# Row numbers by slot in a mixture-of-experts kernel: the tile index moved outside the slot column, 78 columns per product

## Chip, cores and metric

One Trainium2 chip, one core. The time is that of one execution on the device, in microseconds (us), from the median of several executions. Lower is better.

## What is computed

A conditioned layer in front of a mixture of experts, and then a stencil on its result. 2048 tokens of 256 features are normalised twice, scaled and shifted by a style, and routed: each token goes to the two best of eight experts. The part around the change works out only *which token goes where*. Cut to what matters:

```python
h_flat = h.reshape(-1, D)                          # 2048 tokens x 256
probs = softmax(h_flat @ router_w)                 # 8 experts
gates, idx = top_k(probs, 2)
gates = gates / gates.sum(-1, keepdims=True)
combine = zeros((N, E)).at[arange(N)[:, None], idx].add(gates)
hid = relu(einsum('nd,edf->nef', h_flat, exp_w1) + exp_b1)
eout = einsum('nef,efd->ned', hid, exp_w2) + exp_b2
x = x + einsum('ned,ne->nd', eout, combine)
# second layer: a stencil over the 256 x 256 field of each of 8 batches
df = -gradv_Af + gradvv_Bf * 0.5
out = maximum(x + df * dt, 0)
```

## The kernel before

**Stages.** (1) A front part of some 39 us normalises the tokens, turns them, applies the style and writes the result as rows to memory (`h_rows`); the router's logits fall out of the same products. (2) Routing, some 39 to 60 us: the two best experts of each token, its rank within its expert, the expert of each slot, and the row numbers that belong in each slot. (3) The experts: 23 slots, each one expert with up to two tiles of 128 rows. For each slot GpSimd gathers the rows (L731), TensorE turns them (L867) and runs two layers (L891/L893/L898 and L920), and GpSimd scatters the result (L744). The weights are split in a high and a low part by ScalarE and VectorE. (4) The stencil over four pairs of batches.

Each engine has its program written out by hand, with semaphores between them; nothing is reordered by a scheduler.

**The place of the change.** There are 32 tiles of routed tokens (`TOPK * NJ`, two choices times 16 tiles of 128 tokens) and 4992 slot places, 39 columns (`NC`) of 128 rows. At L1142 to L1146 VectorE has the place of each token as a column `col_f` and a row `low_f`. To turn *token to place* round into *place to token*, TensorE multiplies one-hot matrices:

- `oh_col` (L1155): is the column of the token this one? 39 x 32 numbers in each partition, compared with a table `col_of` that GpSimd's iota made (L721).
- `tok` has two halves: `tok[:, 0]` is `oh_col` times the token's number in its tile (ScalarE, L547), `tok[:, 1]` is `oh_col` times 128 times the tile's number (VectorE, L1158).
- `oh_row` (L1162): is the row this one? 128 x 32 numbers, in 4 chunks of 8 tiles.
- L854: for each tile `t` two products, `oh_row[:, :, t]` as weights and the two halves of `tok` at `t` as the 39 moving columns, all 64 added up in one place of PSUM. In all three arrays the tile is the *innermost* index, so that both operands of a product are read with a step of 32 numbers (64 bytes).

TensorE waits for `tok0_ok` (ScalarE), `tok_ok` (VectorE) and, once per 8 tiles, `ohrow_ok`. When all products are done (`perm_mm`), VectorE makes `num_i` and from it `src_cur`, the row numbers of the first two slots (L1169, L1170), on which GpSimd's first gather (L731) waits. `src_i` and `dst_i`, for the later slots, follow. `link` makes an instruction add to a semaphore and lets VectorE wait for it before its next one; `chained` only adds.

```python
dve.tensor_tensor(oh_col[:, :, :], by_tile(col_f[:, :], NC), col_of[:, :, :],
                  ALU.is_equal).then_inc(ohcol_ok, 1)
```

Of the kernel before, what the change touches and what calls it, by code (L numbers as in the profile page):

```python
# [7 lines left out]
ALU = mybir.AluOpType  # L8
# [112 lines left out]
def moe_then_stencil(nc, x, ids, dt, exp_w1, exp_b1, exp_w2, exp_b2, a_grid, b_grid, small, consts, out):  # L121
# [4 lines left out]
    with ctx:  # L126
# [29 lines left out]
        with ExitStack() as phase:  # L156
            def own(name, shape, dt_=F32):
                return phase.enter_context(nc.sbuf_tensor(name, shape, dt_))
# [15 lines left out]
        with ExitStack() as phase:  # L174
            def own(name, shape, dt_=F32):
                return phase.enter_context(nc.sbuf_tensor(name, shape, dt_))

            h_pre = own("h_pre", [P, KD, N])
            hT = own("hT", [P, KD, N])
            own("w_split_first", [P, 10240])  # L180

            z = own("z", [P, 4, D])
            tok = own("tok", [P, 2, NC, TOPK * NJ], BF16)
            own("w_split_last", [P, 6144 - 1024 - TOPK * NJ * NC])
            h_tok = own("h_tok", [P, NJ, KD, P + E])
            oh_row = own("oh_row", [P, P, TOPK * NJ], BF16)
            oh_col = own("oh_col", [P, NC, TOPK * NJ], BF16)
            eye_rw = own("eye_rw", [P, KD, P + E])
            before_bf = own("before_bf", [P, P], BF16)
            ones_bf = own("ones_bf", [P, P], BF16)  # L190
            st1 = own("st1", [P, NJ, 6])
            mv1 = own("mv1", [P, NJ, 2])
            var1 = own("var1", [P, NJ])
            rs1 = own("rs1", [P, NJ])
            st2 = own("st2", [P, NB, KD, 6])
            mv2 = own("mv2", [P, NB, KD, 2])
            var2 = own("var2", [P, NB, KD])
            rs2 = own("rs2", [P, NB, KD])
            half = own("half", [P, 8])
            warm = own("warm", [P, 8])  # L200
            aff_a = own("aff_a", [P, NB, KD])
            aff_m = own("aff_m", [P, NB, KD])
            aff_b = own("aff_b", [P, NB, KD])

            id_i = own("id_i", [S_SUB, NB], I32)
            id_f = own("id_f", [S_SUB, NB])
            oh_s = own("oh_s", [S_SUB, NB])
            small_sb = own("small_sb", [P, SMALL_ALL])
            se_t = own("se_t", [SE, NB])
            hy1 = own("hy1", [SH, NB])  # L210
            hy2 = own("hy2", [SH, NB])
            sy1 = own("sy1", [SH // 2, NB])
            sty = own("sty", [P, 4, NB])
            gabs = own("gabs", [P, KD, NB])
            grelu = own("grelu", [P, KD, NB])
            gexp = own("gexp", [P, KD, NB])
            gln = own("gln", [P, KD, NB])
            gsum = own("gsum", [P, KD, NB])
            gam = own("gam", [P, KD, NB])

            lg = own("lg", [P, NJ, E])
            eq = own("eq", [P, NJ, E])
            cand = own("cand", [P, NJ, E])
            least = own("least", [P, NJ])
            oh = own("oh", [P, TOPK, NJ, E])
            lg2 = own("lg2", [P, NJ, E])
            gap = own("gap", [P, NJ])
            e2 = own("e2", [P, NJ])
            den = own("den", [P, NJ])
            m_bf = own("m_bf", [P, NJ, E], BF16)  # L230
            cnt_i = own("cnt_i", [P, E], I32)
            tl_i = own("tl_i", [P, 2, E], I32)
            tl_f = own("tl_f", [P, 2, E])
            t_end = own("t_end", [P, 2, E])
            t_off = own("t_off", [P, 2, E])
            base = own("base", [P, E])
            room = own("room", [P, E])
            jump = own("jump", [P, E])
            late = own("late", [P, NJ, E])
            pos = own("pos", [P, NJ, E])  # L240
            pick = own("pick", [P, TOPK, NJ, E])
            slot_f = own("slot_f", [P, TOPK * NJ])
            slot_i = own("slot_i", [P, TOPK * NJ], I32)
            low_i = own("low_i", [P, TOPK * NJ], I32)
            col_i = own("col_i", [P, TOPK * NJ], I32)
            low_f = own("low_f", [P, TOPK * NJ], BF16)
            col_f = own("col_f", [P, TOPK * NJ], BF16)
            row_of = own("row_of", [P, P, TOPK * NJ], BF16)
            col_of = own("col_of", [P, NC, TOPK * NJ], BF16)
            tile_of = own("tile_of", [P, TOPK * NJ], BF16)  # L250
            e_cmp = own("e_cmp", [1, 2, NS, E])
            e_sum = own("e_sum", [1, NS])
            num_i = own("num_i", [P, NC], I32)
            num_f = own("num_f", [P, NC])

        def part(name):
            rows, cols, at = SMALL[name]
# [215 lines left out]
        def _(act):  # L473
# [66 lines left out]
            for b in range(3, NB):  # L540
# [3 lines left out]
            act.activation(e2[:, :], gap[:, :], ACT.Exp).then_inc(e2_ok, 1)  # L544

            act.wait_ge(ohcol_ok, 1)
            act.activation(tok[:, 0, :, :], oh_col[:, :, :], ACT.Copy,  # L547
                           scale=cst[:, C_PART + 1:C_PART + 2]).then_inc(tok0_ok, 1)

            def split_w1(k, m, first=False):  # L550
# [150 lines left out]
        def _(pool):  # L701
# [16 lines left out]
                    pool.tensor_tensor(rs2[:, i - 3, :], var2[:, i - 3, :], half[:, 0:KD],  # L718
                                       ALU.pow).then_inc(rs2_ok, 1)
            number(tile_of[:, :], [[P, TOPK * NJ]])  # L720
            number(col_of[:, :, :], [[1, NC], [0, TOPK * NJ]])  # L721
            number(row_of[:, :, :], [[1, P], [0, TOPK * NJ]])

            def gather(k, m):
# [48 lines left out]
        def _(pe):  # L773
# [76 lines left out]
            for t in range(TOPK * NJ):  # L850
                if t % CHUNK == 0:
                    pe.wait_ge(ohrow_ok, t // CHUNK + 1)
                for part in range(2):
                    last = pe.matmul(banks[1][:, 128:128 + NC], oh_row[:, :, t], tok[:, part, :, t],  # L854
                                     start=(t == 0 and part == 0), stop=(t == TOPK * NJ - 1 and part == 1))
            last.then_inc(perm_mm, 1)

            def turn(k, m):
# [114 lines left out]
        def _(dve):  # L973
            steps = [0]

            def link(ins):

                steps[0] += 1
                ins.then_inc(chain, 1)
                dve.wait_ge(chain, steps[0])  # L980
# [168 lines left out]
            TC = TOPK * NJ  # L1149

            def by_tile(v, n):
                return v.rearrange("p (a t) -> p a t", a=1).broadcast_to([P, n, TC])

            dve.wait_ge(iota_ok, 3)
            dve.tensor_tensor(oh_col[:, :, :], by_tile(col_f[:, :], NC), col_of[:, :, :],  # L1155
                              ALU.is_equal).then_inc(ohcol_ok, 1)
            dve.wait_ge(ohcol_ok, 1)
            dve.tensor_tensor(tok[:, 1, :, :], oh_col[:, :, :], by_tile(tile_of[:, :], NC),  # L1158
                              ALU.mult).then_inc(tok_ok, 1)
            for n in range(TC // CHUNK):  # L1160
                at = slice(CHUNK * n, CHUNK * n + CHUNK)
# [2 lines left out]
                    low_f[:, at].rearrange("p (a t) -> p a t", a=1).broadcast_to([P, P, CHUNK]), row_of[:, :, at],  # L1164
                    ALU.is_equal).then_inc(ohrow_ok, 1)
            dve.wait_ge(perm_mm, 1)
            num = banks[1][:, 128:128 + NC]

            link(dve.tensor_scalar(num_i[:, :], num, float(N - 1), None, ALU.add))  # L1169
            dve.tensor_scalar(src_cur[:, :, :], num_i[:, 0:2 * TB].rearrange("p (s t) -> p s t", t=TB), N - 1, None,  # L1170
                              ALU.bitwise_and).then_inc(src_ok, 2)
            dve.tensor_scalar(src_i[:, 0:NC], num_i[:, :], N - 1, None, ALU.bitwise_and)
            dve.memset(src_i[:, NC:NC + TB], 0)

            link(dve.tensor_scalar(num_f[:, :], num, 0.0, EMPTY, ALU.is_equal, ALU.mult))
            link(dve.scalar_tensor_tensor(out=dst_i[:, :], in0=num, scalar=-1.0, in1=num_f[:, :],
                                          op0=ALU.add, op1=ALU.add))

            def source(k, m):
# [229 lines left out]
```

## Time and profile before

| | |
|---|---|
| median of 3 executions | 374.18 us (373.38 to 374.24) |
| the profiled execution | 373.12 us |
| its span, first to last instruction | 371.5 us |
| mean granted TensorE clock in it | 0.938 |
| routing: VectorE's first work on the logits to the start of the first gather | 39.17 to 60.02 us |
| the 64 products of L854 | 53.11 to 58.60 us |

All numbers of a trace are of one execution, counted from the span's start. A share of busy time is an average over stages with different limits; what a piece of the program is worth is read from the chain of waits around it. A row of the timeline gives start, length, engine, line, operation, output and inputs, their shapes, the number of instructions merged in it, and in brackets how long the engine had been idle and what ended that.

### The profile page before, as it was taken

The numbers are of one execution on the slowest core, as the hardware profiler recorded it, in microseconds if no ns is written. First come the engines' busy times: TensorE is split into PE (matmuls) and PEld (weight loads), VectorE is DVE, ScalarE is ACT, GpSimd is POOL, SyncE is SP. The second block draws the span as 40 slices with busy tenths as digits, with TensorE's granted clock in tenths as the row PEclk, the third lists the DMA queues.
The fourth block names the chain that finished last, engine by engine and source line by source line (L and its number), as shares of the span: only waits on it lengthen the run. The fifth ranks groups of instructions, "written<-read, shape, count | busy, mean of one in ns | idle before, by whom it ended". The sixth has DMA issues, their size and how long they took to land.

```text
span 371.5 us, 7201 instructions
## 1 busy us (share of the span) xinstructions
PE 316.9 (85%) x2312; PEld 285.6 (77%) x2312; DVE 290.2 (78%) x521; ACT 253.2 (68%) x463; POOL 145.0 (39%) x108
## 2 busy tenths in 40 slices
PE   1857223799999999999999999999999992399996
PEld 1656223799999999999999999999999992143332
DVE  4988781778878868878887886887887861899993
ACT  2668023597998799789789879978978831568211
POOL 1346204142545555653553554565455142111000
PEclk9999755599999999999999999999999998599999
DMA  8903342985767876765765777787575102987411
GB/s 280 356 0 113 115 182 85 318 296 176 254 250 260 283 268 232 276 243 182 275 244 194 260 265 268 255 277 242 179 241 160 34 18 85 309 187 169 113 57 56
DMA packets 49924, 74.83 MB, mean 201 GB/s; under 512 B 3309, under 2 KB 40559, under 8 KB 49776
## 3 DMA queue, kind: packets, MB, share of 16 engines
q1 hardware_dynamic: 45056, 62.13, 49.0%
q0 software_dynamic: 4512, 12.07, 11.1%
q10 hardware_dynamic: 336, 0.39, 0.3%
q8 instruction: 10, 0.16, 0.2%
q14 instruction: 10, 0.08, 0.1%
HBM read 63.56 MB, written 9.31 MB: 196 GB/s over the span
## 4 chain that ended last, share of the span: by engine, by line
PE 76%; DVE 14%; DMA 4%; issue 2%; POOL 2%; ACT 1%; SPq 0%; DVEq 0%; POOLq 0%
PE psum L920 30%; PE psum L898 25%; PE psum L946 8%; PE psum L891 5%; PE psum L867 2%; PE psum L893 2%; DMA t_y<-y_rows 2%; PE psum L854 1%; DVE st L1017 1%; DVE z L1007 1%; POOL rs L714 1%; DMA x_sb<-in_x_dram 1%; PE psum L814 1%; POOL rs L718 1%; DMA gathered<-h_rows,src_cur 1%
## 5 line engine op out<-in xcount | busy, mean ns | idle before, releaser
L731 POOL DMA_INDIRECT gathered<-h_rows,src_cur x40 | 78.4, 1961 | 123.2 <-DVE src_cur L1183 73.4
L920 PE MATMUL psum<-w_split,hid 128*128 128x256 f32 x936 | 117.8, 285 | 0.2 <-issue 0.2
L920 PEld LDWEIGHTS psum<-w_split,hid 128*128 128x128 f32 x936 | 113.7, 192 | 0.3 <-issue 0.3
L898 PE MATMUL psum<-slot_h,w_split 128*128 128x256 f32 x768 | 97.2, 287 | 2.0 <-DVE slot_h L1200 2.0
L898 PEld LDWEIGHTS psum<-slot_h,w_split 128*128 128x128 f32 x768 | 95.5, 196 | 2.3 <-issue 2.3
L1194 DVE TENSOR_TENSOR w_split<-raw_b,w_split 128x2048 fp32r<-128x2048 f32 x23 | 52.7, 2292 | 22.2 <-ACT w_split L562 21.1
L585 ACT ACTIVATE relu<-psum,b_cur 128x256 f32<-128x256 f32 x128 | 53.4, 484 | 13.0 <-PE psum L898 11.0
L1188 DVE TENSOR_TENSOR w_split<-raw_a,w_split 128x2048 fp32r<-128x2048 f32 x23 | 52.5, 2282 | 8.0 <-DMA gathered<-h_rows,src_cur 7.0
L594 ACT ACTIVATE hid<-relu 128x512 fp32r<-128x512 f32 (+1 forms) x92 | 50.6, 584 | 10.1 <-DVE relu L1206 10.1
L744 POOL DMA_INDIRECT y_rows<-y_sb,dst_cur x39 | 44.7, 1146 | 25.9 <-issue 11.4
L1217 DVE TENSOR_TENSOR hid<-relu,hid 128x512 fp32r<-128x512 f32 x64 | 42.0, 688 | 10.2 <-ACT hid L594 9.5
L562 ACT ACTIVATE w_split<-raw_b 128x2048 fp32r<-128x2048 f32 x23 | 44.5, 1936 | 3.4 <-DMA raw_b<-in_L_cond_exp_w_dram 3.4
L555 ACT ACTIVATE w_split<-raw_a 128x2048 fp32r<-128x2048 f32 x23 | 44.6, 1940 | 2.5 <-DMA raw_a<-in_L_cond_exp_w_dram 2.5
L891 PE MATMUL psum<-slot_h,w_split 128*128 128x256 f32 x112 | 26.3, 332 | 0.0
L893 PE MATMUL psum<-slot_h,w_split 128*128 128x128 f32 x112 | 24.9, 223 | 0.0
L582 ACT ACTIVATE relu<-psum,b_cur 128x128 f32<-128x128 f32 x56 | 17.4, 363 | 7.4 <-PE psum L893 7.1
L893 PEld LDWEIGHTS psum<-slot_h,w_split 128*128 128x128 f32 x112 | 21.5, 192 | 0.0
L891 PEld LDWEIGHTS psum<-slot_h,w_split 128*128 128x128 f32 x112 | 21.1, 189 | 0.0
L946 PE MATMUL psum<-t_kept,cst 128*128 128x512 f32 x16 | 9.4, 719 | 12.7 <-DVE t_kept L1354 12.7
L1200 DVE TENSOR_TENSOR slot_h<-psum,slot_h 128x512 fp32r<-128x512 f32 (+1 forms) x23 | 14.0, 610 | 5.8 <-ACT slot_h L569 3.9
L867 PE MATMUL psum<-cst,gathered 128*128 128x128 f32 x80 | 13.4, 285 | 5.8 <-DMA gathered<-h_rows,src_cur 5.8
L569 ACT ACTIVATE slot_h<-psum 128x512 fp32r<-128x512 f32 (+1 forms) x23 | 12.7, 551 | 6.3 <-PE psum L867 6.3
(166 smaller groups left out, 347.9 us busy)
## 6 DMA issues: line engine op xcount, KB each, us to landing
raw_a<-in_L_cond_exp_w_dram SPq DMA_DIRECT2D x23, 1024.0 KB, 5.8
raw_b<-in_L_cond_exp_w_dram SPq DMA_DIRECT2D x23, 1024.0 KB
t_y<-y_rows SPq DMA_DIRECT2D x6, 512.0 KB, 8.8
x_sb<-t_y POOLq DMA_DIRECT2D x5, 512.0 KB, 4.7
x_sb<-in_x_dram SPq DMA_DIRECT2D x4, 512.0 KB, 6.9
h_rows<-h_tok SPq DMA_DIRECT2D x16, 128.0 KB, 2.2
out_dram<-t_out SPq DMA_DIRECT2D x3, 512.0 KB, 2.9
b_all<-in_L_cond_exp_b_dram SPq DMA_DIRECT2D x1, 1024.0 KB, 9.8
```

The costliest lines, as they stand in the source:

```text
L555: act.activation(w_split[:, 0, par, 0, :], w1_raw[par], ACT.Copy).then_inc(w1_hi, 1)
L562: act.activation(w_split[:, 1, par, 0, :], w2_raw[par], ACT.Copy).then_inc(w2_hi, 1)
L585: last = act.activation(relu[:, bank, i, :], banks[bank][:, ST * i:ST * i + ST], ACT.Relu, bias=bias)
L594: act.activation(hid[:, par, 0, 2 * bank:2 * bank + 2, 0:n], relu[:, bank, :, 0:n], ACT.Relu if width(k) == 1 else ACT.Copy).then_inc(hid_ ...
L731: pool.indirect_dma_start(out=gathered[:, par, t, :], out_offset=None, in_=h_rows, in_offset=bass.IndirectOffsetOnAxis(ap=src_cur[:, par, ...
L744: pool.indirect_dma_start(out=y_rows, out_offset=bass.IndirectOffsetOnAxis(ap=dst_cur[:, par, t:t + 1], axis=0), in_=y_sb[:, par, t, :], i ...
L891: pe.matmul(both, w_split[:, 0, par, 0, at:at + P], slot_h[:, par, :, k, 0:P], start=(k == 0), stop=False)
L893: last = pe.matmul(both[:, 0, :], w_split[:, 0, par, 1, at:at + P], slot_h[:, par, 0, k, 0:P], start=False, stop=(k == KD - 1))
L898: last = pe.matmul(banks[bank][:, ST * (blk % 2):ST * (blk % 2) + rows], w_split[:, 0, par, w, at:at + P], slot_h[:, par, h, k, 0:rows], s ...
L920: last = pe.matmul(banks[bank][:, D * t:D * t + D], hid[:, par, h, blk, P * t:P * t + P], w_split[:, 1, par, w, D * blk:D * blk + D], star ...
L1188: dve.tensor_tensor(w_split[:, 0, par, 1, :], w1_raw[par], w_split[:, 0, par, 0, :].bitcast(F32), ALU.subtract).then_inc(w1_lo, 1)
L1194: dve.tensor_tensor(w_split[:, 1, par, 1, :], w2_raw[par], w_split[:, 1, par, 0, :].bitcast(F32), ALU.subtract).then_inc(w2_lo, 1)
```

## The change

`tok`, `oh_col` and its table `col_of` get the tile index outside and the slot column inside: `tok` is now [tile, half, column]. `oh_row` and `row_of` stay as they are. For each tile there is one product with 78 neighbouring moving columns, both halves side by side, in place of two with 39. The two halves are therefore no longer added up by TensorE: VectorE copies one sum from PSUM to SBUF and adds the other to it, once for `num_i`, and once for a new `num_f` from which `dst_i` is then made.

```diff
-            tok = own("tok", [P, 2, NC, TOPK * NJ], BF16)
+            tok = own("tok", [P, TOPK * NJ, 2, NC], BF16)
-            oh_col = own("oh_col", [P, NC, TOPK * NJ], BF16)
+            oh_col = own("oh_col", [P, TOPK * NJ, NC], BF16)
-            col_of = own("col_of", [P, NC, TOPK * NJ], BF16)
+            col_of = own("col_of", [P, TOPK * NJ, NC], BF16)
...
-            act.activation(tok[:, 0, :, :], oh_col[:, :, :], ACT.Copy,
+            act.activation(tok[:, :, 0, :], oh_col[:, :, :], ACT.Copy,
...
-            number(col_of[:, :, :], [[1, NC], [0, TOPK * NJ]])
+            number(col_of[:, :, :], [[0, TOPK * NJ], [1, NC]])
...
-                for part in range(2):
-                    last = pe.matmul(banks[1][:, 128:128 + NC], oh_row[:, :, t], tok[:, part, :, t],
-                                     start=(t == 0 and part == 0), stop=(t == TOPK * NJ - 1 and part == 1))
+                last = pe.matmul(banks[1][:, 128:128 + 2 * NC].rearrange("p (h c) -> p h c", h=2), oh_row[:, :, t],
+                                 tok[:, t, :, :], start=(t == 0), stop=(t == TOPK * NJ - 1))
...
-                return v.rearrange("p (a t) -> p a t", a=1).broadcast_to([P, n, TC])
+                return v.rearrange("p (t a) -> p t a", a=1).broadcast_to([P, TC, n])
...
-            dve.tensor_tensor(tok[:, 1, :, :], oh_col[:, :, :], by_tile(tile_of[:, :], NC),
+            dve.tensor_tensor(tok[:, :, 1, :], oh_col[:, :, :], by_tile(tile_of[:, :], NC),
                               ALU.mult).then_inc(tok_ok, 1)
...
-            num = banks[1][:, 128:128 + NC]
-
-            link(dve.tensor_scalar(num_i[:, :], num, float(N - 1), None, ALU.add))
+            low, num = banks[1][:, 128:128 + NC], banks[1][:, 128 + NC:128 + 2 * NC]
+
+            link(dve.tensor_copy(num_f[:, :], low))
+            chained(dve.scalar_tensor_tensor(out=num_i[:, :], in0=num, scalar=float(N - 1), in1=num_f[:, :],
+                                             op0=ALU.add, op1=ALU.add))
+            link(dve.tensor_tensor(num_f[:, :], num, num_f[:, :], ALU.add))
...
-            link(dve.tensor_scalar(num_f[:, :], num, 0.0, EMPTY, ALU.is_equal, ALU.mult))
-            link(dve.scalar_tensor_tensor(out=dst_i[:, :], in0=num, scalar=-1.0, in1=num_f[:, :],
+            link(dve.tensor_scalar(num_e[:, :], num_f[:, :], 0.0, EMPTY, ALU.is_equal, ALU.mult))
+            link(dve.scalar_tensor_tensor(out=dst_i[:, :], in0=num_f[:, :], scalar=-1.0, in1=num_e[:, :],
                                           op0=ALU.add, op1=ALU.add))
```

VectorE's order from the one-hot of the columns to the first work for the experts. Before (the shape is that of the output in each partition, a factor at the end counts repeats):

```order
L1155 TENSOR_TENSOR oh_col<-col_f,col_of 128x1248
L1158 TENSOR_TENSOR tok<-oh_col,tile_of 128x1248
L1162 TENSOR_TENSOR oh_row<-low_f,row_of 128x128x8 x4
L1169 TENSOR_SCALAR num_i<-psum 128x39
L1170 TENSOR_SCALAR src_cur<-num_i 128x4
L1172 TENSOR_SCALAR src_i<-num_i 128x39
L1173 MEMSET src_i 128x2
L1175 TENSOR_SCALAR num_f<-psum 128x39
L1176 SCALAR_TENSOR_TENSOR dst_i<-psum,num_f 128x39
L1188 TENSOR_TENSOR w_split<-raw_a,w_split 128x2048
```

and with the change:

```order
L1155 TENSOR_TENSOR oh_col<-col_f,col_of 128x1248
L1158 TENSOR_TENSOR tok<-oh_col,tile_of 128x32x39
L1162 TENSOR_TENSOR oh_row<-low_f,row_of 128x128x8 x4
L1169 COPY num_f<-psum 128x39
L1170 SCALAR_TENSOR_TENSOR num_i<-psum,num_f 128x39
L1172 TENSOR_TENSOR num_f<-psum,num_f 128x39
L1173 TENSOR_SCALAR src_cur<-num_i 128x4
L1175 TENSOR_SCALAR src_i<-num_i 128x39
L1176 MEMSET src_i 128x2
L1178 TENSOR_SCALAR num_e<-num_f 128x39
L1179 SCALAR_TENSOR_TENSOR dst_i<-num_f,num_e 128x39
L1191 TENSOR_TENSOR w_split<-raw_a,w_split 128x2048
```

Two instructions more stand between the products and `src_cur`, and `tok` is written in 32 runs of 39.

TensorE's order at the same place. Before:

```order
L844 MATMUL psum<-m_bf,ones_bf 128x8 x16
L854 MATMUL psum<-tok,oh_row 128x39 x64
L867 MATMUL psum<-cst,gathered 128x128 x4
L898 MATMUL psum<-slot_h,w_split 128x256 x24
```

and with the change:

```order
L845 MATMUL psum<-m_bf,ones_bf 128x8 x16
L854 MATMUL psum<-tok,oh_row 128x78 x32
L867 MATMUL psum<-cst,gathered 128x128 x4
L898 MATMUL psum<-slot_h,w_split 128x256 x24
```

Half the products, each twice as wide; nothing else on TensorE moves.

## Rows read from the trace of the kernel before

**Rows 1.** The page: span, and busy time of each engine.
```profile
span 371.5 us, 7201 instructions
PE 316.9 (85%) x2312; PEld 285.6 (77%) x2312; DVE 290.2 (78%) x521; ACT 253.2 (68%) x463; POOL 145.0 (39%) x108
```

**Rows 2.** Busy time by stretch (columns: length, engines, clock, DMA share, GB/s).
```profile
82.00:284.00 202.00, 202.00 (x1702) 202.00 (x1701) 167.01 (x229) 173.82 (x318) 103.37 (x66) 1.00 0.69 238
```

**Rows 3.** The chain that ended last, in order: start, length, what.
```profile
50.71 0.82 DVE oh_col L1155
51.53 0.02 issue
51.55 0.81 DVE tok L1158
52.36 0.61 DVE oh_row L1162
52.97 0.14 issue
53.11 5.50 PE psum L854 x64
...
58.94 0.18 DVE src_cur L1170
...
61.56 2.84 DMA gathered<-h_rows,src_cur
...
66.68 0.69 DVE slot_h L1200
```

**Rows 4.** Timeline, VectorE and ScalarE ahead of the products, 50.3 to 57.4 us.
```profile
51.55 1.33 ACT L547 ACTIVATE tok<-oh_col,cst 128x1248 bf16<-128x1248 bf16 x1 [7.86 <-DVE oh_col L1155]
52.28 2.49 DVE L1162 TENSOR_TENSOR oh_row<-low_f,row_of 128x1024 bf16<-128x1024 bf16 x4
...
54.92 1.97 ACT L555 ACTIVATE w_split<-raw_a 128x2048 fp32r<-128x2048 f32 x1 [2.03 <-DMA raw_a<-in_L_cond_exp_w_dram]
57.38 1.93 ACT L555 ACTIVATE w_split<-raw_a 128x2048 fp32r<-128x2048 f32 x1 [0.50 <-DMA raw_a<-in_L_cond_exp_w_dram]
```

**Rows 5.** Groups of VectorE by form: busy us, mean ns of one.
```profile
L1188 DVE TENSOR_TENSOR w_split<-raw_a,w_split 128x2048 fp32r<-128x2048 f32 x23 | 52.5, 2282 | 8.0 <-DMA gathered<-h_rows,src_cur 7.0 <-ACT w_split L555 1.0
L1360 DVE TENSOR_TENSOR t_b2f<-gr,t_fd 128x1024 f32<-128x1024 f32 x4 | 4.9, 1220 | 0.1
L1162 DVE TENSOR_TENSOR oh_row<-low_f,row_of 128x1024 bf16<-128x1024 bf16 x4 | 2.5, 684 | 0.0
L1158 DVE TENSOR_TENSOR tok<-oh_col,tile_of 128x1248 bf16<-128x1248 bf16 x1 | 0.8, 807 | 0.0
L1077 DVE TENSOR_TENSOR lg<-h_tok 128x128 f32<-128x128 f32 x1 | 0.3, 294 | 0.1
L1094 DVE TENSOR_TENSOR m_bf<-oh 128x128 bf16<-128x128 f32 x1 | 0.3, 293 | 0.0
```

**Rows 6.** Line L854: duration ns min/median/max, first and last start.
```profile
L854 PEld LDWEIGHTS psum<-tok,oh_row x64: 143/153/179, 53.1 to 58.3; 128*128 128x128 bf16 x64
L854 PE MATMUL psum<-tok,oh_row x64: 249/268/282, 53.1 to 58.3; 128*128 128x39 bf16 x64
```

**Rows 7.** Timeline of TensorE, the ranks: the other bf16 products, weights side by side.
```profile
43.50 1.03 PE L841 MATMUL psum<-m_bf,ones_bf 128*128 128x120 bf16 x15
44.39 0.57 PE L844 MATMUL psum<-m_bf,ones_bf 128*128 128x8 bf16 x16
```

**Rows 8.** Timeline, VectorE behind the products.
```profile
58.63 0.20 DVE L1169 TENSOR_SCALAR num_i<-psum 128x39 int32<-128x39 f32 x1 [3.86 <-PE psum L854]
58.94 0.17 DVE L1170 TENSOR_SCALAR src_cur<-num_i 128x4 int32<-128x4 int32 x1
59.01 0.18 DVE L1172 TENSOR_SCALAR src_i<-num_i 128x39 int32<-128x39 int32 x1
59.11 0.19 DVE L1175 TENSOR_SCALAR num_f<-psum 128x39 f32<-128x39 f32 x1
```

**Rows 9.** Timeline, the first gather and the start of the experts.
```profile
60.02 1.23 POOL L731 DMA_INDIRECT gathered<-h_rows,src_cur  x1 [20.99 <-DVE src_cur L1170]
64.47 2.29 DVE L1188 TENSOR_TENSOR w_split<-raw_a,w_split 128x2048 fp32r<-128x2048 f32 x1 [4.93 <-DMA gathered<-h_rows,src_cur]
```

**Rows 10.** Timeline of GpSimd: the tables.
```profile
33.56 1.35 POOL L707 IOTA col_of<- 128x1248 bf16 x1
```

**Rows 11.** Busy time by stretch, as rows 2: ranks, products, first layer of the experts.
```profile
43.40:45.00 1.60, 1.54 (x32) 1.45 (x32) 0.65 (x4) 0.22 (x1) 0.00 (x0) 0.50 0.28 82
53.10:58.60 5.50, 5.49 (x64) 5.32 (x64) 1.67 (x3) 3.19 (x2) 0.00 (x0) 0.50 0.68 277
67.50:73.00 5.50, 5.49 (x26) 5.50 (x27) 3.01 (x3) 2.60 (x3) 0.42 (x1) 0.50 1.09 363
73.20:82.00 8.80, 8.80 (x75) 8.80 (x75) 6.44 (x8) 8.55 (x18) 3.92 (x3) 1.00 0.97 351
```

More of the change, by code:

```diff
@@ L254, in moe_then_stencil @@
             num_f = own("num_f", [P, NC])
+            num_e = own("num_e", [P, NC])
         def part(name):
```

## The prediction

> **What bounds the kernel now.** I read the page first, for the size of the whole: a span of 371.5 us, TensorE busy 85% of it [rows 1]. The view by stretch then says where it is the bound: from 82 to 284 us, in the loop over the slots, TensorE is busy all the time at full clock [rows 2], so nothing done for VectorE or ScalarE there counts. The change is not in that stretch, though, but in the routing ahead of it, and there the chain of waits is the view to read [rows 3]. Its pieces follow each other without a second path beside them: VectorE's `oh_col`, then its half of `tok`, then the first chunk of `oh_row`; TensorE's 64 products, 5.50 us; VectorE's row numbers up to `src_cur`; GpSimd's gather and its landing; and the first work of the experts. What this chain gains or loses is gained or lost by the start of the loop, and behind it TensorE has no slack to swallow it. So the question is what each edit does between 50.71 us, where `oh_col` starts, and 59.12 us, where `src_cur` is done. For scale: 0.3% of 374.18 us is 1.12 us, about the least difference from no change that a measurement of this kernel can tell. Everything at stake here is of that size.
>
> **Part 1: the one-hot of the columns and VectorE's half of `tok`, ahead of the products.** Both multiply or compare 1248 numbers of two bytes and took 0.807 us each [rows 5]. With the tile outside, the operand that is repeated (`col_f`, `tile_of`) gives the same number 39 times before it steps on; before, it gave 32 neighbouring numbers and then the same 32 again. No row shows such an operand with two-byte numbers, so I bound it. Below: 0.807 us, no change. Above: the rate of the 4-byte rows. `oh_row`, all two-byte and neighbouring, has 1024 numbers in 0.684 us, a 4-byte operation as many in 1.220 us and 2048 in 2.282 us [rows 5], so 1.04 ns for each further number and 1.220 + 224 x 0.00104 = 1.453 us for 1248. I take the upper end, because the fast rate needs every operand in two-byte neighbours: `m_bf` has a two-byte output and 4-byte inputs and took 0.293 us for 128 numbers, no less than the all-4-byte `lg` with 0.294 [rows 5]. A number that is read 39 times over is no pair of neighbours either. That is 0.65 us for each of the two, 1.29 us in all, and both are on the chain.
>
> The Trainium skill bears on this very point ("Vector Engine (DVE) Microarchitecture Reference", 5.1 Performance modes): one element read again and again as an input of a two-source operation with two-byte operands ran at one result per cycle, where rows of neighbours ran at two. By that rule the chain is longer by the 1.29 us just worked out, by the duration in this trace it is not longer at all; the trace of before cannot say which.
>
> ScalarE's half of `tok` starts when `oh_col` is done and took 1.33 us, to 52.88 us; the first chunk of `oh_row` ended at 52.28 + 0.68 = 52.96 us, 0.15 us before the first product [rows 4, 5, 3]. So both arrived together. Now VectorE's half takes 1.45 us instead of 0.81 while ScalarE's still takes 1.33 (it writes runs of 39, for which there is no row: between nothing and the 0.65 us by which VectorE is later behind `oh_col`; anything in that is hidden by VectorE). VectorE alone sets the start of the products: 53.11 + 1.29 = 54.40 us. ScalarE's next work is held by a DMA until 54.92 us [rows 4] and doesn't notice. The table `col_of` is made from 33.56 to 34.91 us [rows 10], 16 us before its use, with as many numbers as before: nothing, and the table `row_of` behind it keeps its place.
>
> **Part 2: the products.** 64 of them start over 5.49 us; the first to the last is 5.49 - 0.25 = 5.24 us, so 83 ns from one to the next [rows 6, 11]. The clock is at half (0.50, 1.2 GHz) [rows 11]. 39 columns at 0.83 ns are only 33 ns. What else is there? The ranks, at the same clock and with weights side by side in memory, have 16 products of 8 columns in 0.57 us, 27 ns from one to the next behind the first's 0.17 [rows 7, 11]: so a weight load from neighbouring memory costs 27 ns at most, and 27 + 33 would be 60, not 83. The step of 64 bytes costs something, in the weights, in the moving columns, or both. The change takes it from the moving columns alone. The bounds for one new product: below, its 78 columns, 65 ns; above, the old 83 ns and the new 65 ns one behind the other, 148 ns. I take 83 ns: the weights are read just as before, and the old pace is the nearest row, since 65 ns of columns fit under it. 31 x 0.083 + 0.25 + 0.03 for the wider last one is 2.86 us instead of 5.49: 2.63 us less.
>
> The Trainium skill has a rule here ("SBUF — State Buffer", Specifications (TRN2)): memory is read in lines of 16 bytes, and an access that meets each line once pays for it. By that the weights, still 64 bytes apart, go on paying, and only the columns are relieved; the sum for a product would then lie between 65 and 83 ns, not above.
>
> The feed stays in time: `oh_row` comes in four chunks in 2.49 us, one each 0.60 us [rows 4, 5], and TensorE eats 8 tiles in 0.66 us where it needed 1.33. That is close: below 75 ns per product VectorE sets the pace.
>
> **Part 3: behind the products.** Today `num_i` starts at 58.63 us and `src_cur` at 58.94 us, 0.31 us for one linked step; an unlinked one follows in 0.07 to 0.10 us [rows 8]. Now a copy is linked (0.31), `num_i` is not waited for but `num_f` behind it is (0.10 + 0.31): `src_cur` starts 0.72 us after the products instead of 0.31, so 0.41 us is added on the chain. `src_i`, `num_e` and `dst_i` come behind `src_cur`, while VectorE would idle 4.93 us for the gather [rows 9]: covered, with some 4.5 us to spare.
>
> **Sum.** +1.29 - 2.63 + 0.41 = **-0.93 us**. GpSimd's gather waits for `src_cur` alone (idle 20.99 us) [rows 9], so it and all behind it move by as much; the weights that it meets landed by 57.4 us [rows 4]. The profiled execution took 373.12 us, so 372.2 for it; the median of the runs is 1.06 us above that execution, so for a median 374.18 - 0.93 = **373.2 us**.
>
> **The rivals.**
> - *VectorE keeps its pace* (the lower bound of part 1). For it: the output and the other input stay neighbours. Against it: `m_bf`. Then -2.63 + 0.41 = -2.22: 372.0 us. 10%.
> - *The moving columns were what was slow.* Then a product costs 65 to 75 ns and TensorE runs at VectorE's pace: three chunks later (1.81 us), 7 x 0.065 and the last 0.28, 2.54 us instead of 2.86, or -1.25: 372.9 us. For it: the step of 64 bytes that goes; against it: nothing tells columns from weights in the rows. 15%.
> - *Half of the gain is lost to the clock.* From 67.5 to 73 us the experts run at half clock (26 products in 5.5 us), behind it at full (75 in 8.8) [rows 11], after TensorE had been busy. If the rise doesn't come earlier with the work, 0.93 us more of it runs at half speed and 0.47 us remain: 373.7 us. For it: nothing ties the rise to a certain product; the runs shown differ by 0.86 us with nothing changed. 13%.
> - *Slower: load and columns don't overlap.* If the 83 ns are all weight load, and the 78 columns stand behind it, a product costs 148 ns: 31 x 0.148 + 0.28 = 4.87 us, only 0.62 less than today, against 1.70 us of added VectorE work: +1.08, 375.3 us. It decides from 113 ns per product, where 31 x 0.113 + 0.28 is 5.49 - 1.70. For it: 83 ns is more than either operand's count of numbers gives; against it: the ranks overlap (products of 120 to 8 columns took 1.03 us for 15, little more than their 960 columns x 0.83 ns [rows 7]). 10%.
>
> That the two halves come out of step with what is computed behind is no rival: they are added again ahead of `num_i`.
>
> **How the numbers follow.** The forecast has 52%, its own range 372.7 to 373.8 (0.5 us, as the runs of before lie around their median). A change counts as faster below 373.06 us, as slower above 375.3. Faster: a third of the forecast's 52%, nearly all of the first rival, two thirds of the second, in all 0.37. Slower: half of the last rival and little of the rest, 0.07. The same: 0.56. The range takes in the first two rivals, the third, and stops in the middle of the last: 371.9 to 374.6 us.
>
> **What the next profile would show.** `oh_col` and VectorE's `tok` at 1.45 us each, `oh_row` unchanged at 0.684; the first product some 3.7 us behind the start of `oh_col` instead of 2.40; 32 products in 2.86 us, 83 ns apart; `src_cur` 0.7 us behind the last of them; 7.5 us from `oh_col`'s start to the end of `src_cur` in place of 8.4. The prediction is wrong in its parts if either of the first two stays at 0.81, if a product takes over 113 ns, or if the stretch before 60 us gains as said and the total does not.

## The result, and the profile after

| | before | changed |
|---|---|---|
| median of 6 executions | 374.21 us (373.38 to 374.38) | 371.57 us (370.85 to 372.45) |
| ratio, 95% interval | | 0.9940 (0.9921 to 0.9959): 2.2 us less (1.5 to 3.0) |
| profiled execution, its span | 373.12, 371.5 us | 370.85, 369.2 us |

The kernel became faster, by more than the 0.93 us of the forecast. The median lies 0.3 us below the lower end of the range, the old median times the ratio, 374.18 x 0.9940 = 371.9, just on it. Two more series of the same kernel, below, gave 1.4 us (0.7 to 2.1) and 1.9 us (1.2 to 2.7). What all three allow is 1.5 to 2.1 us.

The page of the changed kernel, where [rows 1] stood: TensorE has 32 products and 32 weight loads less, VectorE two instructions more and 1.5 us more of work.

```profile
span 369.2 us, 7139 instructions
PE 313.7 (85%) x2280; PEld 282.1 (76%) x2280; DVE 291.7 (79%) x523; ACT 253.1 (69%) x463; POOL 144.5 (39%) x108
```

The chain that ended last, in order of time (start, length, what), the same piece as [rows 3]:

```profile
50.65 1.47 DVE oh_col L1155
52.13 0.02 issue
52.15 1.46 DVE tok L1158
53.61 0.61 DVE oh_row L1162
54.22 0.14 issue
54.36 2.48 PE psum L854 x32
56.83 0.02 issue
56.85 0.21 DVE num_f L1169
...
57.50 0.18 DVE src_cur L1173
...
60.13 2.80 DMA gathered<-h_rows,src_cur
```

The two operations of VectorE went from 0.82 and 0.81 to 1.47 and 1.46 us, the products from 5.50 to 2.48 us, and `src_cur` starts 57.50 - 56.85 = 0.65 us behind them instead of 0.31. From the start of `oh_col` to the start of `src_cur`, a time that I call D from here on, it was 58.94 - 50.71 = 8.23 us; now it is 6.85 us: 1.38 us less.

Line L854 (duration in ns min/median/max, first and last start), against [rows 6]:

```profile
L854 PEld LDWEIGHTS psum<-tok,oh_row x32: 137/168/182, 54.3 to 56.5; 128*128 128x128 bf16 x32
L854 PE MATMUL psum<-tok,oh_row x32: 258/266/286, 54.4 to 56.6; 128*128 128x78 bf16 x32
```

A product of 78 columns lasts 0.266 us, as one of 39 did before (0.268). The first and the last start are 2.46 - 0.27 = 2.19 us apart, 71 ns for each of 31 steps, not the 83 ns that I had kept.

What feeds the products, from the timeline; [rows 4] before:

```profile
52.15 1.38 ACT L548 ACTIVATE tok<-oh_col,cst 128x1248 bf16<-128x1248 bf16 x1 [8.51 <-DVE oh_col L1155]
53.52 2.49 DVE L1162 TENSOR_TENSOR oh_row<-low_f,row_of 128x1024 bf16<-128x1024 bf16 x4
54.36 2.46 PE L854 MATMUL psum<-tok,oh_row 128*128 128x78 bf16 x32 [9.46 <-DVE oh_row L1162]
```

ScalarE's half of `tok` took 1.38 us, 0.05 more than before, and ended at 53.53 us, 0.8 us ahead of the first product: hidden. What one product needs by itself is read from the first seven:

```profile
54.36 0.65 PE L854 MATMUL psum<-tok,oh_row 128*128 128x78 bf16 x7 [9.46 <-DVE oh_row L1162]
```

(0.65 - 0.26) / 6 = 65 ns, 78 columns at 0.83 ns each. The rest of the 71 ns is waiting for VectorE: in the trace the starts lie mostly 63 to 66 ns apart, but 128 and 125 ns where the third and the fourth chunk of `oh_row` begin. VectorE's last chunk ends at 53.52 + 2.49 = 56.01 us. The old hand-over from a chunk to a product took 0.14 us; from there 8 products at 65 ns and the last one's 0.27 end at 56.15 + 7 x 0.065 + 0.27 = 56.88 us, where the burst in fact ended at 56.82. So it is VectorE's pace of 0.60 us a chunk that TensorE keeps now.

What came behind followed. By stretch (length, TensorE, its weight loads, VectorE, ScalarE, GpSimd, clock, DMA share, GB/s), first of the kernel before:

```profile
60.00:73.10 13.10, 6.71 (x30) 6.34 (x31) 6.00 (x5) 3.50 (x6) 4.64 (x5) 0.50 0.70 217
73.20:76.00 2.80, 2.80 (x25) 2.80 (x25) 2.64 (x3) 2.63 (x7) 2.26 (x1) 1.00 1.02 407
```

and of the changed one:

```profile
60.00:71.70 11.70, 6.76 (x30) 6.39 (x31) 5.89 (x5) 3.39 (x6) 3.42 (x4) 0.50 0.77 247
71.80:76.00 4.20, 4.20 (x37) 4.20 (x36) 3.45 (x4) 4.01 (x10) 2.37 (x1) 1.00 1.02 403
```

TensorE's clock rose behind the same 30 products, at 73.1 us then and 71.7 us now. Further on, the chains of both at the end of the expert loop. Before:

```profile
309.06 0.44 DVE y_sb L1236
...
313.84 5.63 DMA t_y<-y_rows
```

and changed:

```profile
307.68 0.44 DVE y_sb L1239
...
311.96 4.40 DMA t_y<-y_rows
```

The last result of the experts is ready 1.38 us earlier, just what D lost (`src_cur` itself starts 1.44 us earlier, since `oh_col` starts 0.06 us earlier too). The spans differ by 2.3 us. The other 0.9 us is a sum of three: the load of the experts' results starts 4.28 us behind the last result instead of 4.78, it takes 4.40 us instead of 5.63, and what follows it takes 0.8 us more. The experiments tell whether the load belongs to the change.

### The profile page after: what moved, and what is told of

Same layout as the page of the kernel before. It is cut to its first block, busy times and chain, and to the rows that moved or that the text cites. A ratio compares the mean times of both kernels' runs of the same rounds, so it can differ in the third digit from the quotient of the medians.

```text
span 369.2 us, 7139 instructions
## 1 busy us (share of the span) xinstructions
PE 313.7 (85%) x2280; PEld 282.1 (76%) x2280; DVE 291.7 (79%) x523; ACT 253.1 (69%) x463; POOL 144.5 (39%) x108
## 4 chain that ended last, share of the span: by engine, by line
PE 76%; DVE 15%; DMA 4%; issue 2%; POOL 2%; ACT 1%; SPq 0%; DVEq 0%; POOLq 0%
PE psum L920 30%; PE psum L898 26%; PE psum L946 8%; PE psum L891 5%; PE psum L867 2%; PE psum L893 2%; DVE st L1017 1%; DVE z L1007 1%; DMA t_y<-y_rows 1%; POOL rs L715 1%; DMA x_sb<-in_x_dram 1%; PE psum L815 1%; POOL rs L719 1%; DMA gathered<-h_rows,src_cur 1%; PE psum L854 1%
## 5 line engine op out<-in xcount | busy, mean ns | idle before, releaser
L745 POOL DMA_INDIRECT y_rows<-y_sb,dst_cur x39 | 43.5, 1115 | 27.1 <-issue 11.4
L803 PE MATMUL psum<-cst,z 128*128 128x128 f32 x32 | 8.1, 409 | 9.6 <-DVE z L1007 9.6
```

The source lines that it names most:

```text
L745: pool.indirect_dma_start(out=y_rows, out_offset=bass.IndirectOffsetOnAxis(ap=dst_cur[:, par, t:t + 1], axis=0), in_=y_sb[:, par, t, :], i ...
```

## The experiments

Two questions were open after the result. Why does a product take 65 ns and not 83: which of its two operands was slow? And does the gain end at `src_cur`, or does something behind add to it? In the short diffs, lines of the changed kernel have a minus; where a base is another kernel, it is said.

### Layout alone, and width alone

**Two products of 39 columns in the new layout.**

```diff
-                last = pe.matmul(banks[1][:, 128:128 + 2 * NC].rearrange("p (h c) -> p h c", h=2), oh_row[:, :, t],
-                                 tok[:, t, :, :], start=(t == 0), stop=(t == TOPK * NJ - 1))
+                for part in range(2):
+                    last = pe.matmul(banks[1][:, 128:128 + NC], oh_row[:, :, t], tok[:, t, part, :],
+                                     start=(t == 0 and part == 0), stop=(t == TOPK * NJ - 1 and part == 1))
...
```

> The layout of the change (tile outside), but again two products of 39 neighbouring columns per tile, added up by TensorE in one place, and the row numbers made as before; nothing is left out. Theory W (the read of the weights, 64 bytes apart, sets the pace of the products): 64 products at some 70 ns, 4.5 us of products, so about 2.0 us longer there than in the changed kernel and 0.4 us shorter behind. Theory C (the strided columns set the pace): 64 products at 33 ns, so the burst lasts as long as VectorE takes to feed it, 2.3 to 2.5 us, and the kernel is 0.4 us faster than the changed one.

Measured: 373.23 us, ratio to before 1.0006 (0.9986 to 1.0025). The timeline of TensorE in it:

```profile
54.76 4.15 PE L855 MATMUL psum<-tok,oh_row 128*128 128x39 bf16 x64 [9.46 <-DVE oh_row L1163]
```

A burst less its last product's own time, by the number of steps, is the time from one product to the next: (4.15 - 0.23) / 63 = 62 ns. Theory W is the nearer one: with its columns side by side a product falls from 83 ns only to 62, though 39 columns are 33 ns, so something else holds it there, by theory W the weights, 64 bytes apart; the runs with these side by side, below, bear that out. D is 8.19 us (51.06 to 59.25). The layout alone takes 1.34 us off the burst and puts 1.30 on VectorE: nothing is left.

**One product of 78 columns in the old layout** (base: the kernel before).

```diff
-                for part in range(2):
-                    last = pe.matmul(banks[1][:, 128:128 + NC], oh_row[:, :, t], tok[:, part, :, t],
-                                     start=(t == 0 and part == 0), stop=(t == TOPK * NJ - 1 and part == 1))
+                last = pe.matmul(banks[1][:, 128:128 + 2 * NC].rearrange("p (h c) -> p h c", h=2), oh_row[:, :, t],
+                                 tok[:, :, :, t], start=(t == 0), stop=(t == TOPK * NJ - 1))
...
```

> The layout of before (tile inside), but one product per tile with 78 columns, 64 bytes apart, and the row numbers made as in the change; nothing is left out. Theory W: 32 products at 70 to 85 ns, 2.5 to 2.8 us of products, oh_col and tok at 0.81 us each, src_cur about 1.3 us earlier than in the changed kernel. Theory C: 32 products at some 165 ns, 5.3 us, src_cur about 1.5 us later than in the changed kernel.

Measured: 372.87 us, ratio 0.9986 (0.9965 to 1.0008). The timeline of TensorE in it:

```profile
53.42 4.87 PE L854 MATMUL psum<-tok,oh_row 128*128 128x78 bf16 x32 [8.16 <-DVE oh_row L1162]
```

(4.87 - 0.31) / 31 = 147 ns. Here theory C is the nearer: columns 64 bytes apart cost 1.9 ns each, over twice their 0.83. Each theory had named a part. Half the number of products alone saves 0.62 us on TensorE and pays 0.33 for the sum on VectorE: D is 7.95 us (51.02 to 58.97), 0.28 less. Neither half of the change moves the total by more than its interval allows for chance; together they take 1.38 us off D.

### The missing corner

**Weights side by side, columns still apart** (base: the kernel before). `oh_row` and its table have the tile outside. To keep VectorE's pace the row number of each token stands twice, side by side.

```diff
-            oh_row = own("oh_row", [P, P, TOPK * NJ], BF16)
-            row_of = own("row_of", [P, P, TOPK * NJ], BF16)
-            low_f = own("low_f", [P, TOPK * NJ], BF16)
+            oh_row = own("oh_row", [P, TOPK * NJ, P], BF16)
+            row_of = own("row_of", [P, TOPK * NJ, P], BF16)
+            low_f = own("low_f", [P, TOPK * NJ, 2], BF16)
...
-                    oh_row[:, :, at],
-                    low_f[:, at].rearrange("p (a t) -> p a t", a=1).broadcast_to([P, P, CHUNK]), row_of[:, :, at],
+                    in_twos(oh_row[:, at, :]), paired(low_f[:, at, :], P), in_twos(row_of[:, at, :]),
```

`paired` repeats [tile, 2] as [tile, n / 2, 2], so that the innermost two are neighbours; `in_twos` writes the other operands in the same shape.

> The kernel before the change, and only oh_row and its table in neighbours (tile outside, row number of each token twice); the moving columns stay 39 and 64 bytes apart. The missing corner: columns apart and weights apart cost 83 ns a product, columns side by side and weights apart 60 to 62, both side by side 33. If the columns alone set the old pace: 63 to 83 ns, a burst of 4.2 to 5.4 us. If the two add up (27 more ns for the weights): near 55 ns and 3.7 us. Total 0.1 to 1.8 us below the kernel before.

Measured: 372.18 us, ratio 0.9971 (0.9953 to 0.9989). Line L854 of it (duration in ns min/median/max, first and last start):

```profile
L854 PEld LDWEIGHTS psum<-tok,oh_row x64: 104/124/126, 53.7 to 58.0; 128*128 128x128 bf16 x64
L854 PE MATMUL psum<-tok,oh_row x64: 227/246/248, 53.7 to 58.1; 128*128 128x39 bf16 x64
```

The burst is 4.58 us, (4.58 - 0.25) / 63 = 69 ns, and a weight load is recorded with 124 ns instead of 153. So the columns alone hold a product at 69 ns, the weights alone at 62, both together at 83: neither a sum nor just the slower of the two. D is 7.32 us (51.35 to 58.67), 0.91 less than before, and the whole kernel 1.1 us faster (0.4 to 1.8), by this edit alone. The expectation "the columns alone set the old pace" is the nearer, at its lower end.

### VectorE's pace in the new layout, and everything side by side

**Paired numbers.** As above, now for `col_f`; the tile numbers become a full table, made by GpSimd in the front part; rows are padded to 40 columns.

```diff
-            dve.tensor_tensor(oh_col[:, :, :], by_tile(col_f[:, :], NC), col_of[:, :, :],
+            dve.tensor_tensor(in_twos(oh_col[:, :, :]), paired(col_f[:, :, :], NCP), in_twos(col_of[:, :, :]),
                               ALU.is_equal).then_inc(ohcol_ok, 1)
...
-            dve.tensor_tensor(tok[:, :, 1, :], oh_col[:, :, :], by_tile(tile_of[:, :], NC),
+            dve.tensor_tensor(tok[:, :, 1, :], oh_col[:, :, :], tile_of[:, :, :],
```

> The changed kernel with VectorE's fast pace kept in the new layout: the column number of each token stands twice side by side, so that the repeated operand is read in neighbouring twos, the tile numbers are a full table made by GpSimd in the front part, and rows are padded to 40. D is the time from the start of oh_col to the start of src_cur: 8.23 us before, 6.85 us with the change. Theory (the repeated single number halves VectorE's rate, 2 x 0.65 us on the chain): oh_col and VectorE's tok at 0.82 us each, D 5.6 us, total 1.25 us below the changed kernel. Rival (ScalarE's half then holds the products, or the writing of tok in runs costs VectorE as much): tok stays at 1.4 us or the products start no earlier than 2.9 us behind oh_col, D above 6.2 us.

Measured: 370.04 us, ratio 0.9915 (0.9894 to 0.9935). Its timeline, VectorE, ScalarE and TensorE:

```profile
50.66 0.83 DVE L1162 TENSOR_TENSOR oh_col<-col_f,col_of 128x1280 bf16<-128x1280 bf16 x1
51.52 0.83 DVE L1165 TENSOR_TENSOR tok<-oh_col,tile_of 128x1280 bf16<-128x1280 bf16 x1
51.53 1.36 ACT L549 ACTIVATE tok<-oh_col,cst 128x1280 bf16<-128x1280 bf16 x1 [7.88 <-DVE oh_col L1162]
53.10 2.45 PE L855 MATMUL psum<-tok,oh_row 128*128 128x78 bf16 x32 [8.20 <-DVE oh_row L1169]
```

As the theory said: both operations are back at 0.83 us for 1280 numbers, with the tile still outside. Writing in runs did not halve the rate: `tok` is written in runs here too, and in the changed kernel `oh_col`, which is written in one piece, was as slow as `tok`. That leaves the single number repeated. The padding came in by the same edit, though: no run has rows of 40 with a single number repeated, so a part played by the odd length 39 is not excluded. D is 5.57 us (50.66 to 56.23), 1.28 less than with the change.

**The same, with two products of 39.**

```diff
-                last = pe.matmul(banks[1][:, 128:128 + 2 * NC].rearrange("p (h c) -> p h c", h=2), oh_row[:, :, t],
-                                 tok[:, t, :, 0:NC], start=(t == 0), stop=(t == TOPK * NJ - 1))
+                for part in range(2):
+                    last = pe.matmul(banks[1][:, 128:128 + NC], oh_row[:, :, t], tok[:, t, part, 0:NC],
+                                     start=(t == 0 and part == 0), stop=(t == TOPK * NJ - 1 and part == 1))
```

> As the kernel with paired numbers, but two products of 39 neighbouring columns per tile and the row numbers made as before the change; the weights are still 64 bytes apart. If the read of the weights holds a product at 62 ns whatever the columns: 64 products in 4.15 us, D 6.95 us. It is the partner of the next one.

Measured: 371.40 us, ratio 0.9948 (0.9928 to 0.9968). The burst is 3.99 us, (3.99 - 0.22) / 63 = 60 ns a product, and D is 6.77 us (50.76 to 57.53). Its timeline, TensorE:

```profile
53.19 3.99 PE L856 MATMUL psum<-tok,oh_row 128*128 128x39 bf16 x64 [8.21 <-DVE oh_row L1170]
```

**Everything side by side**: to this the `oh_row` of the missing corner.

```diff
-                    last = pe.matmul(banks[1][:, 128:128 + NC], oh_row[:, :, t], tok[:, t, part, 0:NC],
+                    last = pe.matmul(banks[1][:, 128:128 + NC], oh_row[:, t, :], tok[:, t, part, 0:NC],
...
```

> As the one with two products of 39 and paired numbers, and oh_row and its table also get the tile outside and the row inside (the row number of each token twice), so that the weights are 128 neighbours. Theory W2 (weights 64 bytes apart cost 62 ns to load, neighbours 27): products at 33 to 38 ns, held by VectorE's four chunks, burst 2.5 us, D 5.3 us, total 1.5 us below the changed kernel and the fastest so far. Rival (62 ns was something of the 39-column product itself): 4.15 us again, D 6.95 us.

Measured: 369.38 us, ratio 0.9899 (0.9880 to 0.9918). Its timeline from `oh_row` to `src_cur`:

```profile
52.34 2.49 DVE L1170 TENSOR_TENSOR oh_row<-low_f,row_of 128x1024 bf16<-128x1024 bf16 x4
53.17 2.43 PE L856 MATMUL psum<-tok,oh_row 128*128 128x39 bf16 x64 [8.22 <-DVE oh_row L1170]
55.63 0.20 DVE L1176 TENSOR_SCALAR num_i<-psum 128x39 int32<-128x39 f32 x1 [0.81 <-PE psum L856]
55.94 0.17 DVE L1177 TENSOR_SCALAR src_cur<-num_i 128x4 int32<-128x4 int32 x1
```

(2.43 - 0.20) / 63 = 35 ns a product: in the trace 33 to 34 ns within a chunk, the time of 39 columns, and up to 90 ns where TensorE waits for the next one. Theory W2 holds: with the weights side by side the 60 ns are gone. D is 5.21 us. It beats the changed kernel twice over: VectorE keeps its pace, and since TensorE adds the halves again, the sum on VectorE goes too. Once more, for its interval:

> The kernel with everything in neighbours once more, for its interval: ratio 0.990 to 0.992, 3.0 to 3.8 us below the kernel before.

Measured: 369.48 us, ratio 0.9903 (0.9878 to 0.9929); D 5.20 us again.

**GpSimd makes the tile half of `tok`.**

```diff
+            pool.wait_ge(ohcol_ok, 1)
+            pool.tensor_tensor(tok[:, :, 1, :], oh_col[:, :, :], tile_of[:, :, :], ALU.mult).then_inc(tok_ok, 1)
...
-            dve.tensor_tensor(tok[:, :, 1, :], oh_col[:, :, :], tile_of[:, :, :],
-                              ALU.mult).then_inc(tok_ok, 1)
```

> As the one with everything in neighbours, and the tile half of tok is made by GpSimd beside ScalarE's half instead of by VectorE, which goes on to oh_row at once. If GpSimd needs no more than ScalarE's 1.33 us for 1280 numbers: D 5.0 us, 0.3 us less. If it needs over 1.7 us the products start later than with VectorE and D is above 5.3 us; no row shows GpSimd at this kind of work.

Measured: 370.55 us, ratio 0.9930 (0.9910 to 0.9950), a loss of 1.2 us against its base. Its timeline, the three engines:

```profile
51.53 4.89 DVE L1170 TENSOR_TENSOR oh_row<-low_f,row_of 128x1024 bf16<-128x1024 bf16 x4
51.76 2.91 POOL L727 TENSOR_TENSOR tok<-oh_col,tile_of 128x1280 bf16<-128x1280 bf16 x1 [11.96 <-DVE oh_col L1166]
54.77 2.43 PE L859 MATMUL psum<-tok,oh_row 128*128 128x39 bf16 x64 [9.77 <-POOL tok L727]
```

GpSimd took 2.91 us, to 54.67 us, and TensorE started 0.10 us behind it, 1.6 us later than with VectorE's half; D is 6.75 us (50.78 to 57.53) instead of 5.21. VectorE's four chunks took 4.89 us in place of 2.49, but not evenly. Line L1170 (duration in ns min/median/max, first and last start), and its second chunk in the timeline:

```profile
L1170 DVE TENSOR_TENSOR oh_row<-low_f,row_of x4: 678/682/3090, 51.5 to 55.7; 128x1024 bf16<-128x1024 bf16 x4
52.13 3.09 DVE L1170 TENSOR_TENSOR oh_row<-low_f,row_of 128x1024 bf16<-128x1024 bf16 x1
```

The first chunk took its usual 0.69 us, though GpSimd worked beside the last 0.45 of them. The second came while GpSimd was at work and ended 0.55 us behind it, after 3.09 us; the other two took 0.68 each. So VectorE was not slowed throughout: one operation was held for 2.4 us. That GpSimd held it fits these times, but no run tests it.

### Does the gain end at `src_cur`?

**The changed kernel, delayed**: VectorE's half of `tok` is computed a second time into a buffer that nobody reads, ahead of the real one.

```diff
+            dve.tensor_tensor(idle_w[:, :, :], oh_col[:, :, :], by_tile(tile_of[:, :], NC), ALU.mult)
             dve.tensor_tensor(tok[:, :, 1, :], oh_col[:, :, :], by_tile(tile_of[:, :], NC),
```

> The changed kernel with VectorE's half of tok computed once more, into a buffer that nobody reads, just ahead of the real one: some 1.4 us of delay on the chain, which puts src_cur back to where it was before the change (58.9 us). Theory of a plain shift: the total is 1.4 us above the changed kernel (373.0), and the rest of the gain, 0.8 us or more, comes from something that does not hang on this time. Theory of a later amplifier (clock or a collision of transfers that hangs on when the experts start): the total is back at 374.2.

Measured: 373.11 us, ratio to before 1.0000 (0.9986 to 1.0014); D is 8.21 us (51.32 to 59.53). Its chain of waits:

```profile
51.32 1.47 DVE oh_col L1156
...
52.81 1.46 DVE idle_w L1159
54.27 1.37 DVE tok L1160
...
56.39 2.48 PE psum L855 x32
...
59.53 0.18 DVE src_cur L1175
```

With D back at its old value, the total is back too: to 0.14% either way, some 0.5 us, the change is worth nothing but its D. That speaks against a gain that doesn't hang on this time. It doesn't decide between a plain shift and one with something added behind, since both expectations (373.0 and 374.2) were written from the first series, whose kernel before ran 0.9 us slower than here. Against the changed kernel of its own series (372.04 us, below) the delay cost 1.1 us, for 1.36 us of D.

**The changed kernel twice more.**

> The changed kernel once more, for a second profile and more executions. If the 1.0 us that the profiled execution gained behind the experts (the first loads of the experts' results, 5.63 before and 4.40 us after) belongs to the change, this load is again near 4.4 us; if it is chance of one execution, it lies anywhere between 4.4 and 5.7 us. Median within 0.3 us of 371.6.

Measured: 372.04 us, ratio 0.9963 (0.9945 to 0.9982), so 1.4 us less than before.

> The changed kernel a third time, to narrow the size of its gain: the first series gave 2.2 us (1.5 to 3.0), the second 1.4 us (0.7 to 2.1), the trace says 1.44 us at src_cur. If the trace tells all: a ratio of 0.9962. If something behind adds to it: 0.994.

Measured: 371.31 us, ratio 0.9949 (0.9928 to 0.9969), so 1.9 us less. D was 6.85 us in both. The load of the experts' results took 5.18 and 4.32 us. The chain of the first of them:

```profile
312.74 5.18 DMA t_y<-y_rows
```

and of the other:

```profile
313.37 4.32 DMA t_y<-y_rows
```

In the profiles of the other kernels it lay between 4.26 and 7.23 us, and the longest, 7.23, belongs to a kernel that is faster than before. It is the chance of one execution. The 0.9 us by which the two profiles differ beyond 1.38 are no effect of the change that one could show.

Up to there the shift is plain. In the 13 profiles `src_cur` starts anywhere from 55.94 to 59.53 us, and the last result of the experts (`y_sb`) starts 249.6 to 250.2 us behind it, 250.1 in the kernel before and 250.2, 250.1 and 250.0 in the changed one. The rest of the span is 62.4 us in the kernel before and 61.5, 61.9 and 61.5 us in the changed one, and from 61.3 to 62.5 in the others: 62.5 with a D of 6.77 us (paired numbers, two products of 39), 61.8 with one of 8.21 (the delayed kernel).

Whether the medians gain a few tenths more than D (1.4, 1.9 and 2.2 against 1.4) stays open: each interval is 1.4 or 1.5 us wide, and the second and the third hold 1.38, the first does not.

## Why the prediction was right, and where it was not

- **What bounds, and where the change acts:** right. D lost 1.38 us, and the last result of the experts came 1.38 us earlier.
- **Part 1, VectorE, +1.29 us:** right. 1.453 us was worked out for each operation, 1.460 and 1.457 were measured. The upper bound was the one to take, and the reason given, that a number read 39 times over is no pair of neighbours, fits the experiment: with the numbers paired (and the rows padded to 40) both operations took 0.83 us. The rival *VectorE keeps its pace* fell. ScalarE's runs of 39 cost 0.05 us, hidden.
- **Part 2, the products, -2.63 us:** the step that failed. "I take 83 ns: the weights are read just as before, and the old pace is the nearest row, since 65 ns of columns fit under it." 83 ns was the pace of *two* slow reads together, and it was not kept once one of them was mended. With the columns side by side the weights hold a product at 60 to 62 ns, below the 65 ns of its 78 columns. The burst took 2.46 us, not 2.86: the term is 2.46 - 5.49 = -3.03 us. That is the rival *the moving columns were what was slow*, with 15%: it gave 2.54 us for the burst, through the same mechanism, VectorE's chunks setting the pace. Its words were not quite right either: the weights were slow as well, only less so than 78 columns are long.
- **Part 3, the sum on VectorE, +0.41 us:** right in kind, 0.34 measured (0.65 against 0.31). The linked copy took 0.24 us, not the 0.31 of the step that I had read it from.
- **Sum:** the first product came 3.71 us behind the start of `oh_col` instead of 2.40, so +1.31 - 3.03 + 0.34 = -1.38 us, just what D lost. So the mechanism was right and one term mis-sized, by 0.4 us of 0.93. The 56% for "the same", by the prediction's own line at 373.06 us, went to the wrong side: the median is 371.57 us.
- **The rival of the clock** (0.47 us lost) fell in the profiled pair: the rise came 1.4 us earlier with the work. It is not bound to the work, though: counted from the experts' first product on `slot_h`, it came after 5.6 and 5.7 us in this pair, after 3.9 and 3.7 in the other two profiles of the changed kernel, and in all 13 between 3.1 (the missing corner) and 5.9 (paired numbers, two products of 39). It is worth little: from `src_cur` to the last result of the experts it took 250.1 to 250.2 us where the rise came after 5.6 us or more, and 249.6 to 250.1 where it came within 4.4.
- **The slower rival** (148 ns, load and columns one behind the other) fell: with the columns side by side no kernel's mean was above 71 ns.
- **The two rules of the Trainium skill.** The Trainium skill ("Vector Engine (DVE) Microarchitecture Reference", 5.1 Performance modes) has a two-source operation with two-byte operands at one result per cycle when one element is read again and again: the trace agrees, 1.46 us in place of 0.81. The Trainium skill ("SBUF — State Buffer", Specifications (TRN2)) has reads in 16-byte lines, and a price for each new line. The runs agree in kind: 78 columns 64 bytes apart took 147 ns, side by side 65. The prediction had put a product between 65 and 83 ns by it, and the burst shows 71. The costs of the two operands neither add up nor hide behind one another: 69 and 60 to 62 ns alone, 83 together.

## What to carry to other kernels

A product reads two operands, and each can be the slow one: before you forecast what mending one of them brings, bound the pace by the *other's* own time, not by the old pace of both. Put what TensorE reads side by side, and keep VectorE's two-byte pace by writing a value that is to be repeated twice next to itself; the layout that serves the reader need not cost the writer. And where an edit moves work from one engine to another, look for whom the faster engine now waits: here 32 or 64 products took the same 2.4 us, because four chunks of VectorE feed them. And moving work to an idle engine is no gain where that engine needs longer: GpSimd took 2.91 us for what VectorE did in 0.83, and the kernel lost 1.2 us.

## What the runs showed of the hardware that I had not expected

- bf16 products at half clock, mean time from one to the next with 39 columns: both operands 64 bytes apart 83 ns, only the columns apart 69, only the weights apart 62 (rows of 39) or 60 (rows padded to 40), neither 35 (33 to 34 where VectorE doesn't hold it). 78 columns, weights apart: columns apart 147, side by side 65.
- Worked out from these, one column 64 bytes from the next costs 69 / 39 = 1.8 to 147 / 78 = 1.9 ns, side by side 65 / 78 = 0.83.
- GpSimd beside VectorE: 1280 two-byte products took GpSimd 2.91 us, where VectorE needs 0.83. Of VectorE's four comparisons at the same time one took 3.09 us and the others 0.68 to 0.69, as usual: a wait of one operation, not a slower pace.
